# Attention with rotary embedding: rotated rows are transposed unstacked and spread by DMA, TensorE's steps are evened, GpSimd forms the cosine product from batch 1 on

## The chip, the cores and the metric

The kernel runs on one core of a Trainium2 chip. The metric is the device time of one execution in microseconds (us).

## What is computed

The program is a chain of two blocks, each an attention and a feed-forward part. The change lies in the first attention alone: four batches (B = 4) of 512 tokens (S = 512) with a width of 256, as 16 heads of 16 dimensions.

```
qkv = (x @ Wqkv + bqkv).reshape(b, s, 3, H, hd)
q, k, v = (qkv[:, :, 0], qkv[:, :, 1], qkv[:, :, 2])
...
def rot(t):
    t1, t2 = jnp.split(t.astype(jnp.float32), 2, axis=-1)
    return jnp.concatenate([t1 * c - t2 * si, t1 * si + t2 * c], axis=-1).astype(x.dtype)
q = rot(q)
k = rot(k)
scores = jnp.einsum('bthd,bshd->bhts', q, k * scale)
attn = jax.nn.softmax(scores + causal_mask, axis=-1)
ctx = jnp.einsum('bhts,bshd->bthd', attn, v).reshape(b, s, d)
return ctx @ Wout + bout
```

## The kernel before

Everything named here is in `attention_stage`. Each engine has a program of its own, written out by hand; semaphores tie them together. After a start-up for batch 0, all engines walk through one common numbering of steps `t`, 96 steps for the scores (`ALL`) and a few more for what trails. A pair of heads (a window `w`) takes three steps, a batch takes eight windows, so `WIDTH` = 24 steps; `u` is the step within the batch. In step `t`:

- TensorE multiplies one third of a window's scores (`scores`, into two PSUM banks, one for each head of the pair), VectorE adds the causal mask and takes the negative row maxima (`maxima`). `scores` of a head waits until the maxima of that head's previous step are taken.
- Seven steps later (`LAG`) TensorE multiplies the scores again, transposed, with the shift by the maximum as a 49th row of the contraction (`shifted`); ScalarE exponentiates them (`exponentials`), GpSimd zeroes what lies above the diagonal (`keep_causal`, one step later), and TensorE weighs the values (`weigh`, in two of every six steps).
- Beside it the next batch is prepared (`front`): transposing the normalised tokens (`turn_x`), `project_qk` and `project_v` (seven matmuls each), rotary embedding (`rope_a`, `swapped`, `rotate`). The batch before is finished (`tail`): `turn_sums`, `normalise_sums`, `turn_context`, `project_half`, `add`.

Products keep nearly fp32 precision by a split: a number is a high part (fp32r) and a low rest, and a head's contraction of 48 rows holds (high, low, high) of q against (high, high, low) of k. Before the change these 64-wide stacks are made ahead of the transposition: ScalarE writes the high parts (`high`), GpSimd the rests (`low`), into `q_stack` and `k_stack`; VectorE's maxima go into column 48 of `q_stack`. `turn_stack` then transposes four blocks of 128x128 for each of three things in a window: q without its shift (`turn_q1`), k (`turn_k`), and q again with its shift (`turn_q2`). ScalarE copies q out of PSUM twice (`out_q1`, `out_q2`), VectorE copies k (`out_k`).

The SP queue in this stage only loads rows at its start and stores `x` and the normalised rows.

## Time and profile before

| | us |
|---|---|
| median of 3 runs | 1167.31 (1165.92 to 1172.52) |
| profiled execution, its time | 1165.93 |
| its span, first to last instruction | 1164.0 |
| TensorE busy, whole span | 1052.2 |
| first scores of the attention loop issued at | 236.65 |

The span is what the rows below share as a time axis; the time of an execution is slightly longer than its span. "Busy" on TensorE includes the modelled tail of a matmul, in which the next one already streams, so the mean duration of a matmul is not its price: the price is the distance from one start to the next.

### The profile page before, as it was taken

What the parts mean: (1) busy time and instruction counts of PE and PEld (TensorE: products, weight loads), DVE (VectorE), ACT (ScalarE), POOL (GpSimd) and SP (SyncE); (2) the same over time, 40 slices, a digit from 0 to 9 for tenths busy, and PEclk for the clock granted to TensorE, in tenths of its full rate; (3) what the DMA queues carried; (4) which work ended last, traced back from release to release, by engine and by line L of the source; (5) the groups of instructions that cost most, each with busy time, mean ns of one, the idle gap of its engine ahead of it and who ended that gap; (6) DMA issues with size and microseconds to landing.
All of it is one profiled execution on the core that took longest, in us unless ns stands there. A gap on an engine that the chain in (4) does not pass through costs nothing. (4 is left out here: it accounts for less than half of the span.)

```text
span 1164.0 us, 18769 instructions
## 1 busy us (share of the span) xinstructions
PE 1052.2 (90%) x6537; PEld 870.1 (75%) x6537; DVE 731.1 (63%) x1754; ACT 463.2 (40%) x806; POOL 432.6 (37%) x474
## 2 busy tenths in 40 slices
PE   4899995779999999987999987999988998899997
PEld 3778884656566665666888886888878897788886
DVE  7934443787777778557454446765648878555653
ACT  4324331327666756625243322233334434223222
POOL 3056654326362723201576521000139788300000
PEclk8699998889989998887999998999997999999999
DMA  9034422300000000117472241000010030000000
GB/s 335 31 94 144 156 80 90 108 0 2 2 1 20 1 19 19 37 37 290 143 252 91 83 162 61 1 1 1 1 73 1 4 70 1 1 1 19 19 19 19
DMA packets 36881, 72.39 MB, mean 62 GB/s; under 512 B 8180, under 2 KB 25654, under 8 KB 36536
## 3 DMA queue, kind: packets, MB, share of 16 engines
q1 hardware_dynamic: 29112, 50.21, 12.8%
q0 software_dynamic: 7680, 20.98, 5.5%
q8 instruction: 57, 0.93, 0.3%
q14 instruction: 32, 0.26, 0.1%
HBM read 47.04 MB, written 24.13 MB: 61 GB/s over the span
## 5 line engine op out<-in xcount | busy, mean ns | idle before, releaser
L2041 PE MATMUL ps<-xt,w 128*128 128x512 f32 x768 | 192.5, 401 | 7.0 <-PEq L66 7.0
L2041 PEld LDWEIGHTS ps<-xt,w 128*128 128x128 f32 x768 | 143.3, 192 | 36.9 <-issue 5.5
L1740 DVE CUSTOM_DVE_ANT_0 ps<-ps,att_mask 128x128 f32<-128x128 f32 (+3 forms) x256 | 119.1, 516 | 40.6 <-PE ps L1343 40.3
L718 PE MATMUL ps<-moe_w,moe_narrow_xb 128*128 x480 | 125.0, 395 | 0.0
L122 POOL TENSOR_TENSOR var_eps<-bn,eps 128x4 f32<-128x4 f32 x24 | 6.6, 275 | 290.5 <-DVE bn L99 265.5
L2137 DVE TENSOR_TENSOR had_gated<-ps,had_sig 128x512 f32<-128x512 f32 x64 | 44.3, 691 | 110.8 <-ACT had_sig L2094 110.8
L2094 ACT ACTIVATE had_sig<-ps 128x512 f32<-128x512 f32 x64 | 38.3, 598 | 188.7 <-PE ps L2041 188.7
L616 POOL DMA_INDIRECT moe_xs<-xn_rows,moe_index x80 | 80.7, 1009 | 75.5 <-DVE moe_index L1017 44.1
L622 POOL DMA_INDIRECT made_rows<-moe_units_made,moe_index x80 | 79.6, 994 | 74.6 <-ACT moe_units_made L845 62.1
L718 PEld LDWEIGHTS ps<-moe_w,moe_narrow_xb 128*128 128x128 f32 x480 | 90.1, 188 | 19.6
L1606 ACT ACTIVATE att_early_probs<-ps 128x384 f32<-128x384 f32 (+1 forms) x192 | 90.7, 527 | 29.4 <-PE ps L1358 28.5
L1245 POOL TENSOR_SCALAR_AFFINE_SELECT att_early_probs<-att_early_probs 128x256 f32<-128x256 f32 x128 | 53.5, 431 | 118.1 <-ACT att_early_probs L1606 118.0
L1036 DVE TENSOR_TENSOR moe_narrow_xb<-ps,moe_narrow_xb 128x512 fp32r<-128x512 f32 x40 | 27.6, 691 | 110.2 <-ACT moe_narrow_xb L827 110.1
L2055 PE MATMUL ps<-w,had_yhi 128*128 128x256 f32 x512 | 94.4, 283 | 1.8 <-DVE had_ylo L2149 1.8
L2055 PEld LDWEIGHTS ps<-w,had_yhi 128*128 128x128 f32 x512 | 82.9, 189 | 7.8 <-DVE had_ylo L2149 2.6
L827 ACT ACTIVATE moe_narrow_xb<-ps 128x512 fp32r<-128x512 f32 x40 | 23.8, 598 | 135.0 <-PE ps L702 135.0
L1343 PE MATMUL ps<-att_kt,att_q 48*128 48x256 f32 (+3 forms) x256 | 66.4, 417 | 11.8 <-DVE att_q_stack L1740 9.1
L2055 PE MATMUL ps<-w,had_ylo 128*128 128x256 f32 x256 | 72.2, 282 | 0.0
L2277 POOL TENSOR_TENSOR fea_inv_norm<-fea_norm,neg_half 128x24 f32<-128x24 f32 x16 | 66.7, 4172 | 11.3 <-DVE fea_norm L2506 11.1
L337 PE MATMUL ps<-column,ident 128*128 128x128 f32 x356 | 53.5, 320 | 18.3 <-PEq L66 11.1
L744 PE MATMUL ps<-moe_w,moe_units_yb 128*128 x480 | 67.6, 280 | 0.0
L337 PEld LDWEIGHTS ps<-column,ident 128*128 128x128 f32 x356 | 51.7, 234 | 19.8 <-issue 11.2
(276 smaller groups left out, 2320.0 us busy)
## 6 DMA issues: line engine op xcount, KB each, us to landing
moe_w<-in_moe SPq DMA_DIRECT2D x16, 768.0 KB, 8.9
back<-made_rows SPq DMA_DIRECT2D x16, 512.0 KB, 5.7
x<-x_turned SPq DMA_DIRECT2D x8, 512.0 KB, 7.9
low_weights<-moe_w SPq DMA_DIRECT2D x4, 768.0 KB, 3.6
moe_w<-low_weights SPq DMA_DIRECT2D x4, 768.0 KB, 16.7
x<-in_x SPq DMA_DIRECT2D x4, 512.0 KB, 5.5
xn_rows<-moe_wide_xn SPq DMA_DIRECT2D x4, 512.0 KB, 10.7
x_turned<-x SPq DMA_DIRECT2D x4, 512.0 KB, 2.9
```

The source lines that it names most:

```text
L337: nc.tensor.matmul(g.ps[:, bank, 0:P], g.ident[:, :], g.column[:, :], start=True, stop=True)
L616: nc.gpsimd.indirect_dma_start(out=xs[:, j % AHEAD, i, :], out_offset=None, in_=g.xn_dram[:, :], in_offset=at(0, 2 * j + i)).then_inc(gath ...
L622: nc.gpsimd.indirect_dma_start(out=g.made_dram[:, :], out_offset=at(1, 2 * j + i), in_=made[:, j % 2, i, :], in_offset=None) \
L718: last = nc.tensor.matmul(h_bank(j, i), xb[a][:, j % 2, i, k, :], weight(c), start=False, stop=(k == KC - 1 and c == 1))
L744: last = nc.tensor.matmul(O_BANK[:, i * D:(i + 1) * D], yb[a][:, j % 2, i, c, :], weight(q), start=False, stop=(c == IC - 1 and q == 1), s ...
L1245: last = nc.gpsimd.affine_select(block, block, [[0, 2], [1, P]], ALU.is_ge, 0.0, base=0, channel_multiplier=-1)
L1343: last = nc.tensor.matmul(g.ps[:, a, col:col + n], q1[at, w % 2, i * P:n], kt[at, w % 4, 0:n], start=True, stop=True)
L1606: nc.scalar.activation(probs[:, w % 3, a, at:at + n], g.ps[:, 2 + a, 0:n], ACT.Exp, scale=HD ** -0.5).then_inc(exp_done, 1)
L1740: last = nc.vector.tensor_tensor_reduce(g.ps[:, a, col:col + n], g.ps[:, a, col:col + n], mask[:, SEQ - n:SEQ], -1.0, 3.0e38, ALU.add, ALU ...
L2041: last = nc.tensor.matmul(g.ps[:, bank(n, half), :], w[a][:, k, c * P:(c + 1) * P], xt[low][:, b % 2, k, :], start=(k == 0 and q == 0), st ...
L2055: last = nc.tensor.matmul(o, a[:, n % 4, at], g.w2[w][:, c, :], start=(c == 0 and q == 0 and i % 2 == 0), stop=(c == HC - 1 and q == 2), s ...
L2277: nc.gpsimd.tensor_tensor(inv_norm[:, t % 4, :], norm2[:, t % 4, :], g.neg_half[:, 0:QKH], ALU.pow) \
```

## The change

The rotated rows stay as they are (`rot`, 128 tokens x 512 columns for each of four token tiles). A chunk is 128 columns of them, that is eight heads of q or of k, so a batch has four chunks (q and k of heads 0 to 7, q and k of heads 8 to 15). `turn_chunk` transposes a chunk as it is (four blocks of 128x128), ScalarE takes the high part and VectorE the rest (`high_chunk`, `low_chunk`) into `stage`, SP stores both to DRAM (`store_chunk`, two DMAs) and loads them back spread over the 48 rows of the two heads of each pair (`load_chunk`, six DMAs), into `qt` and `kt`. The first pair's rows of batch 0 are placed from `stage` directly. The maxima go into a small tile `shift`; four matmuls with an identity turn them into two rows (`turn_shift`), ScalarE copies these out (`out_shift`), and SP places each into row 48 of `qt` (`place_shift`, two DMAs for a window). `shifted` waits for that landing. `WIDTH`, `LAG` and the products themselves stay.

Besides, projections are cut in pieces over several steps, `weigh` splits three blocks to one instead of two to two, `project_v` fills one PSUM bank with two tiles, and from batch 1 on GpSimd forms the product with the cosines, in place in `qk`, behind its two products with the sines. In batch 0 GpSimd takes the sine products, which VectorE took before, and VectorE keeps the cosine product. The ones in `kt` are set by two GpSimd memsets of 4096 columns (`set_ones`), the second behind the sine products of batch 0. Norm statistics of batch `b + 2` move from step 19 to step 5, their use from 22 to 7; `store_x` and `store_xn` of batches 0 and 1 move to fixed steps in SP's list.

```diff
-        rot = turns("rot", [P, 2, 2 * D])
...
-        part_b = sb("part_b", [P, 2, 2 * D])
+        rot = sb("rot", [P, BT, 2 * D])
+        stage = sb("stage", [P, 2, 2, SEQ], F32R)
+        shift = sb("shift", [P, 3, BT, 2], F32R)
+        shift_row = sb("shift_row", [P, SEQ], F32R)
+        ident_r = sb("ident_r", [P, P], F32R)
         v = sb("v", [P, 2, BT, H, HD + 1])
-        q_stack = sb("q_stack", [P, 2, BT, H, SK], F32R)
-        k_stack = sb("k_stack", [P, 2, BT, H, SK], F32R)
-        q1 = sb("q1", [P, 2, SEQ], F32R)
-        q2 = sb("q2", [P, 2, SEQ], F32R)
-        kt = sb("kt", [P, 4, SEQ], F32R)
+        qt = sb("qt", [P, 2, H // 2, SEQ], F32R)
+        kt = sb("kt", [P, 2, H // 2, SEQ], F32R)
         inv_sum = sb("inv_sum", [P, BT, H])
...
+        COPIES = ((0, 1, 0), (0, 0, 1))
+        CHUNK_BANK = 4
+        LEAD_CHUNKS = 2
+        stacked = (qt, kt)
+
+        CHUNK_TURNS = {2: 2, 5: 3}
+        for b in range(1, BATCH):
+            begin = WIDTH * (b - 1)
+            CHUNK_TURNS.update({begin + 17: 4 * b, begin + 18: 4 * b + 1, begin + 23: 4 * b + 2, begin + 26: 4 * b + 3})
+
...
+        def shift_turned_at(t):
+            return (t - 4) // STEPS if t >= 4 and (t - 4) % STEPS == 0 and (t - 4) // STEPS < BATCH * PAIR else None
...
+            def store_chunk(n):
+                b, c = n // 4, n % 4
+                sp.wait_ge(chunk_hi, n + 1)
+                sp.wait_ge(chunk_lo, n + 1)
+                if b:
+                    sp.wait_ge(rows_here[c], 96 * b)
+                for half in range(2):
+                    sp.dma_start(g.spread_dram[c, half], f32(stage[:, n % 2, half, :])).then_inc(stage_stored[n % 2], 16)
+
+            def load_chunk(n):
+                b, c = n // 4, n % 4
+                begin = 1 if n < LEAD_CHUNKS else 0
+                sp.wait_ge(stage_stored[n % 2], 32 * (n // 2 + 1))
+                sp.wait_ge(ones_set, min(b, 1) + 1)
+                if b >= 2:
+                    sp.wait_ge(st_ps, 2 * STEPS * PAIR * (b - 1))
+                for a, rows, half in copies(n):
+                    mine = g.spread_dram[c, half].rearrange("(m a d) n -> a d m n", a=2, d=HD)[a]
+                    sp.dma_start(f32(stacked[n % 2][rows, b % 2, 4 * (c // 2) + begin:4 * (c // 2) + 4, :]),
+                                 mine[:, begin:, :]).then_inc(rows_here[c], 16)
+
+            def place_shift(w):
+                b, hp = w // PAIR, w % PAIR
+                sp.wait_ge(shift_out, w + 1)
+                for a in range(2):
+                    at = 64 * a + 3 * HD
+                    sp.dma_start(f32(qt[at:at + 1, b % 2, hp, :]), f32(shift_row[a:a + 1, :])).then_inc(shift_here, 16)
...
+            for t in range(ALL + LAG):
+                if shift_turned_at(t - 1) is not None:
+                    place_shift(shift_turned_at(t - 1))
+                if t - 2 in CHUNK_TURNS:
+                    load_chunk(CHUNK_TURNS[t - 2])
+                if t - 1 in CHUNK_TURNS:
+                    store_chunk(CHUNK_TURNS[t - 1])
+                if t in BESIDE:
+                    store, b = BESIDE[t]
+                    store(b)
...
+                if n >= BT:
+                    pool.wait_ge(b_done, n + 1)
+                    heads = qk[:, n % 2, :].rearrange("p (h d) -> p h d", d=HD)
+                    nc.gpsimd.tensor_tensor(heads, heads, rope_c[:, n % BT, :].unsqueeze(1).to_broadcast([P, 2 * H, HD]),
+                                            ALU.mult).then_inc(a_done, 1)
...
-            def low(n):
-                pool.wait_ge(hi_done, n + 1)
-                b, i = n // BT, n % BT
-                halves = rot[:, n % 2, :].rearrange("p (s h d) -> p s h d", s=2, d=HD)
-                for s, (stack, hi, lo) in enumerate(((q_stack, 0, 1), (k_stack, 0, 2))):
-                    last = nc.gpsimd.tensor_tensor(stack[:, b % 2, i, :, lo * HD:(lo + 1) * HD], halves[:, s, :, :],
-                                                   f32(stack[:, b % 2, i, :, hi * HD:(hi + 1) * HD]), ALU.subtract)
-                last.then_inc(lo_done, 1)
...
+            def turn_rows(n, i):
+                kind, half = n % 2, n % 4 // 2
+                at = kind * D + half * P
+                return nc.tensor.transpose(g.ps[:, chunk_bank(n), i * P:(i + 1) * P], rot[:, i, at:at + P], g.ident[:, :])
+
...
+            def turn_shift(w, t):
+                pe.wait_ge(cleared, 2)
                 pe.wait_ge(max_done, 2 * STEPS * (w + 1))
+                pe.wait_ge(chunk_hi, chunks_turned(t))
+                pe.wait_ge(chunk_lo, chunks_turned(t))
+                if w:
+                    pe.wait_ge(shift_out, w)
+                for i in range(BT):
+                    last = nc.tensor.matmul(g.ps[0:2, CHUNK_BANK, i * P:(i + 1) * P], shift[:, w % 3, i, :],
+                                            ident_r[:, :], start=True, stop=True)
+                last.then_inc(shift_ps, 1)
...
-                    pe.wait_ge(q2_out, w + 1)
+                    pe.wait_ge(shift_here, 32 * (w + 1))
...
+            for i in range(BT):
+                project_v(0, i, 5 + i // 2)
+                pe.wait_ge(rot_done, i + 1)
+                for n in range(LEAD_CHUNKS):
+                    last = turn_rows(n, i)
+                    if i == BT - 1:
+                        last.then_inc(chunk_ps, 1)
+            spin(nc, g, 1, 13)
+            pe.wait_ge(chunk_lo, LEAD_CHUNKS)
...
+                        weigh((t - 14) // 6, 1)
                     elif (t - 14) % 6 == 1:
-                        weigh((t - 14) // 6, 1)
                         weigh((t - 14) // 6, 0)
-                if step == 0 and s + 1 < BATCH * PAIR:
-                    turn_q1(s + 1)
-                elif step == 1 and s + 1 < BATCH * PAIR:
-                    turn_k(s + 1)
-                elif step == 2 and 1 <= s <= BATCH * PAIR:
-                    turn_q2(s - 1)
...
-                        project_qk(front, 0, 6)
+                        project_qk(front, 0, 6, range(0, 1))
                     elif u == 4:
-                        project_qk(front, 1, 5)
+                        project_qk(front, 0, 6, range(1, 4))
+                    elif u == 5:
+                        project_qk(front, 0, 6, range(4, 7))
+                        project_qk(front, 1, 5, range(0, 3))
+                    elif u == 6:
...
+                if shift_turned_at(t) is not None:
+                    turn_shift(shift_turned_at(t), t)
+                if t in CHUNK_TURNS:
+                    turn_chunk(CHUNK_TURNS[t], t)
...
+            def high_chunk(n):
+                act.wait_ge(chunk_ps, n + 1)
+                if n >= 2:
+                    act.wait_ge(stage_stored[n % 2], 32 * (n // 2))
+                if LEAD_CHUNKS <= n < 2 * LEAD_CHUNKS:
+                    act.wait_ge(direct_here[n % 2], 96)
+                nc.scalar.activation(stage[:, n % 2, 0, :], g.ps[:, chunk_bank(n), :], ACT.Copy).then_inc(chunk_hi, 1)
+
+            def out_shift(w):
+                act.wait_ge(shift_ps, w + 1)
+                if w:
+                    act.wait_ge(shift_here, 32 * w)
+                nc.scalar.activation(shift_row[0:2, :], g.ps[0:2, CHUNK_BANK, :], ACT.Copy).then_inc(shift_out, 1)
...
-            def out_k(w):
-                dve.wait_ge(k_ps, w + 1)
-                if w >= 4:
-                    dve.wait_ge(st_ps, 2 * STEPS * (w - 3))
-                nc.vector.tensor_copy(kt[:, w % 4, :], g.ps[:, 4, :]).then_inc(k_out, 1)
+            def low_chunk(n):
+                dve.wait_ge(chunk_hi, n + 1)
+                nc.vector.tensor_tensor(stage[:, n % 2, 1, :], g.ps[:, chunk_bank(n), :], f32(stage[:, n % 2, 0, :]),
+                                        ALU.subtract).then_inc(chunk_lo, 1)
...
+                if t - 1 in CHUNK_TURNS:
+                    low_chunk(CHUNK_TURNS[t - 1])
```

TensorE in batch 2, from the last weighing of a group of heads in step `u` = 3 on (`L1373`/`L1454` weigh, `L1343`/`L1422` are scores, `L1358`/`L1439` shifted scores, `L1294`, `L1297`/`L1362`, `L1365` a projection). Before:

```order
L1373 MATMUL ps<-att_early_probs_4139,att_v 17x512 x4
L1313 MATMUL ps<-ident,att_q_stack 128x128 x4
L1294 MATMUL ps<-att_b_row,ones 128x512
L1297 MATMUL ps<-wqkv0,att_xt0 128x512
L1297 MATMUL ps<-wqkv1,att_xt0 128x512
L1297 MATMUL ps<-wqkv0,att_xt1 128x512
L1297 MATMUL ps<-wqkv0,att_xt0 128x512
L1297 MATMUL ps<-wqkv1,att_xt0 128x512
L1297 MATMUL ps<-wqkv0,att_xt1 128x512
L1343 MATMUL ps<-att_kt,att_q1 128x384 x2
L1358 MATMUL ps<-att_q2,att_kt 128x512 x2
L1313 MATMUL ps<-ident,att_k_stack 128x128 x4
```

After, from the same place (`L1401` is `turn_shift`):

```order
L1454 MATMUL ps<-att_early_probs_4139,att_v 17x512 x4
L1362 MATMUL ps<-att_b_row,ones 128x512
L1422 MATMUL ps<-att_kt,att_qt 128x384 x2
L1439 MATMUL ps<-att_qt,att_kt 128x512 x2
L1365 MATMUL ps<-wqkv0,att_xt0 128x512
L1365 MATMUL ps<-wqkv1,att_xt0 128x512
L1365 MATMUL ps<-wqkv0,att_xt1 128x512
L1401 MATMUL ps<-att_ident_r,att_shift 2x128 x4
L1422 MATMUL ps<-att_kt,att_qt 128x512 x2
L1439 MATMUL ps<-att_qt,att_kt 128x384 x2
L1365 MATMUL ps<-wqkv0,att_xt0 128x512
L1365 MATMUL ps<-wqkv1,att_xt0 128x512
```

The transposes of `q_stack` and `k_stack` are gone, a projection that stood whole in one step is spread over three, and four matmuls with two columns (`att_shift`) are new.

The SP queue between its loads and the end of the stage. Before:

```order
L330 DMA back_49<-made_rows 128x4x256 x6
L1182 DMA x_turned0<-x 128x4x256 x2
L1186 DMA xn_rows<-att_turns_after_xn_4143 128x4x256 x2
L1182 DMA x_turned0<-x 128x4x256
L1186 DMA xn_rows<-att_turns_after_xn_4143 128x4x256
```

After, from the rows of maxima in batch 0 that follow its own chunks to the first steps of batch 2 (`spread_rows` is the DRAM tensor, `att_shift_row` the row of maxima):

```order
L1235 DMA att_qt<-att_shift_row 1x16x32 x10
L1216 DMA spread_rows<-att_stage 128x512 x2
L1227 DMA att_qt<-spread_rows 16x4x512 x6
L1216 DMA spread_rows<-att_stage 128x512 x2
L1235 DMA att_qt<-att_shift_row 1x16x32 x2
L1227 DMA att_kt<-spread_rows 16x4x512 x6
L1235 DMA att_qt<-att_shift_row 1x16x32 x2
L1216 DMA spread_rows<-att_stage 128x512 x2
L1227 DMA att_qt<-spread_rows 16x4x512 x6
L1235 DMA att_qt<-att_shift_row 1x16x32 x2
L1239 DMA x_turned0<-x 128x4x256
L1216 DMA spread_rows<-att_stage 128x512 x2
```

Where SP had only stores that nothing in the loop waits for, it now issues in one list the chunks' stores and loads and the rows of maxima; a load waits for its store to land, and what stands behind it waits with it.

## Rows read from the trace of the kernel before

**Rows 1.** The page, part 1: busy time of each engine, whole span.
```profile
PE 1052.2 (90%) x6537; PEld 870.1 (75%) x6537; DVE 731.1 (63%) x1754; ACT 463.2 (40%) x806; POOL 432.6 (37%) x474
```

**Rows 2.** Windows: the fourth batch of the attention loop, and the loop whole.
```profile
core 0: us, PE busy (x) PEld busy (x) DVE busy (x) ACT busy (x) POOL busy (x), PEclk, DMA share, GB/s
...
420.00:480.00 60.00, 57.27 (x419) 35.19 (x411) 46.72 (x181) 34.85 (x71) 15.69 (x38) 0.89 0.08 28
237.00:481.70 244.70, 231.40 (x1627) 151.19 (x1626) 186.54 (x662) 152.50 (x312) 98.80 (x176) 0.92 0.03 10
```

**Rows 3.** Waits inside the loop, 237 to 481.7 us: waiter, awaited, us, times, longest.
```profile
DVE ps L1740 <- PE ps L1343: 40.3, 35, 3.5
...
PE ps L1343 <- DVE att_q_stack L1740: 9.1, 19, 3.1
```

**Rows 4.** Groups of instructions, 215 to 520 us.
```profile
L1313 PE MATMUL ps<-ident,att_q_stack 128*128 128x128 f32 x256 | 45.6, 305 | 1.8 <-DVE att_kt L1730 1.3
...
L1313 PE MATMUL ps<-ident,att_k_stack 128*128 128x128 f32 x128 | 22.4, 301 | 1.1 <-ACT att_q L1590 0.7
L1730 DVE CAST att_kt<-ps 128x512 fp32r<-128x512 f32 x32 | 21.9, 685 | 1.4 <-PE ps L1313 1.3
L1225 POOL TENSOR_TENSOR att_part_b<-att_qk,att_rope_s 128x256 f32<-128x256 f32 x24 | 20.5, 875 | 16.0 <-ACT att_qk L1566 16.0
...
L1590 ACT ACTIVATE att_q<-ps 128x512 fp32r<-128x512 f32 x32 | 19.2, 599 | 33.6 <-PE ps L1313 33.6
...
L1716 DVE TENSOR_TENSOR att_turns_rot<-att_qk,att_rope_c 128x512 f32<-128x512 f32 x16 | 12.2, 762 | 3.4 <-ACT att_qk L1566 3.4
...
L1708 DVE TENSOR_TENSOR att_xt<-ps,att_xt 128x512 fp32r<-128x512 f32 x6 | 4.1, 686 | 1.8 <-ACT att_xt L1558 1.8
```

**Rows 5.** Timeline of TensorE, four pieces in batch 1.
```profile
309.44 0.66 PE L1313 MATMUL ps<-ident,att_k_stack 128*128 128x128 f32 x4
309.85 0.48 PE L1294 MATMUL ps<-att_b_row,ones 128*128 128x512 f32 x1
310.17 1.56 PE L1297 MATMUL ps<-wqkv,att_xt 128*128 128x512 f32 x6
311.65 0.50 PE L1343 MATMUL ps<-att_kt,att_q 48*128 48x512 f32 x2
```

**Rows 6.** Windows: two neighbouring stretches of the loop, and one around rows 5.
```profile
268.00:271.40 3.40, 2.56 (x18) 1.83 (x16) 3.36 (x10) 1.91 (x5) 3.40 (x6) 0.94 0.00 0
271.40:274.80 3.40, 3.40 (x17) 2.68 (x16) 2.40 (x11) 2.19 (x6) 2.58 (x5) 0.56 0.00 0
308.80:312.20 3.40, 3.40 (x20) 2.23 (x19) 2.41 (x7) 2.12 (x4) 1.44 (x2) 1.00 0.00 0
```

**Rows 7.** Timeline at the start-up: VectorE, GpSimd and the first scores.
```profile
208.48 1.79 DVE L1804 SCALAR_TENSOR_TENSOR x<-back,route,x 128x256 f32<-128x256 f32 x4
...
230.95 4.31 DVE L1804 SCALAR_TENSOR_TENSOR x<-back,route,x 128x256 f32<-128x256 f32 x4
...
232.05 2.53 POOL L1215 TENSOR_TENSOR x<-x,att_bout 128x1024 f32<-128x1024 f32 x1
...
236.65 0.50 PE L1343 MATMUL ps<-att_kt,att_q 48*128 48x128 f32 x4 [0.88 <-DVE att_kt L1730]
```

**Rows 8.** DMA issues: KB each, us from issue to landing.
```profile
back<-made_rows SPq DMA_DIRECT2D x16, 512.0 KB, 5.7
...
low_weights<-moe_w SPq DMA_DIRECT2D x4, 768.0 KB, 3.6
...
x_turned<-x SPq DMA_DIRECT2D x4, 512.0 KB, 2.9
...
route<-route_rows SPq DMA_DIRECT2D x1, 16.0 KB, 1.9
```

**Rows 9.** Timeline of the SP queue: one DMA issued.
```profile
485.21 0.36 SPq L1182 DMA_DIRECT2D x_turned<-x  x1
```

376 lines of the change are left out of this document (167 added, 209 removed).

## Prediction

> **What bounds the kernel now.** I read the page's busy shares first: TensorE is busy for 1052.2 of 1164.0 us [rows 1]. That is an average over stages, and the change touches one, so the next view is the windows of that stage. The attention loop, from the first maxima to the last, takes 244.7 us for 96 steps, 2.55 us a step; in it TensorE is busy for 231.4 us, VectorE for 186.5, ScalarE for 152.5, GpSimd for 98.8 [rows 2]. The waits say who waits for whom: VectorE's maxima wait 40.3 us for scores, TensorE's scores wait only 9.1 us for maxima [rows 3]. So TensorE is what ends last in most steps, and VectorE, busy for 76% of the loop, is next. The granted clock averages 0.92 over the loop [rows 2], that is, a part of it runs at 1.2 instead of 2.4 GHz. A reader should see two things here: work taken from TensorE counts, and it counts only until VectorE, or a wait that is new, is last.
>
> **What TensorE loses.** 256 transposes of the q stack and 128 of the k stack go [rows 4]. Their mean of 0.3 us is not their price, since matmuls overlap: four transposes start at 309.44 and the next matmul at 309.85, so one costs 0.41 / 4 = 0.103 us [rows 5], at a granted clock of 1.00 [rows 6]. 384 x 0.103 = 39.4 us at full clock, 42.8 at the loop's 0.92.
>
> **What TensorE gains.** 64 transposes of chunks, 56 of them inside the loop: 56 x 0.103 = 5.8 us. 128 matmuls for the shift, 128 columns moving and 2 columns of weights, which the trace does not show. Above they are bounded by the transpose (0.103), below by the streaming of 128 columns: six matmuls of 512 columns take 311.65 - 310.17 = 1.48 us [rows 5], 0.247 each, a quarter of which is 0.062. I take 0.062, since the weights are short: 7.9 us (13.2 at most). Together 13.7 us, 14.9 at 0.92. Net: 42.8 - 14.9 = 27.9 us less (22 at least).
>
> **Does VectorE take over?** It loses 32 copies of k at 0.685 us, 21.9 us, and 12 cosine products at 0.762, 9.1 us, and gains 14 rests of a chunk in the loop, which I cost as the rests of x at 0.686, 9.6 us [rows 4]. That is 21.4 us less, 165.1 us of work. In a loop of 244.7 - 27.9 = 216.8 us its share is 76%, as before, so the full cut should show unless something new waits. ScalarE trades 64 copies of 0.6 us [rows 4] for 32 of the rows of maxima and 14 of chunks, and drops the writing of the stacks; it has room and I cost it at nothing. Its cover is that it sits idle for a third of the loop.
>
> **New wait one: chunks through PSUM.** A chunk is turned at the end of a step; ScalarE's copy takes 0.60 us, VectorE's rest 0.69 [rows 4], and in VectorE's list that rest stands ahead of the step's maxima, for which the next scores wait. So VectorE stands for 0.60 us and then works 0.69 us ahead of the maxima. A step will be about 216.8 / 96 = 2.26 us long and TensorE has its own work in it. Bounds: nothing, or all 1.29 us for 14 chunks, 18 us. I take 0.3 us each, 4 us, because one step of slack lies between scores and maxima.
>
> **New wait two: SP's list.** Nothing in the loop hung on SP before; now `shifted` waits for a row of maxima placed by DMA. Undisturbed, the row needs 0.60 for the copy, two issues at 0.36 each [rows 9] and 1.9 to land (a 16 KB transfer [rows 8]), 3.2 us from the end of the step that turned it. It is wanted two steps and the next scores later, after some 4.6 us. So it is hidden with 1.4 us to spare. A load of a chunk is six issues, 2.2 us, and it waits until the chunk's store (512 KB, 2.9 us [rows 8]) has landed, so some 5 us after the turn; the row of maxima then queues behind six issues and is 2.2 - 1.4 = 0.8 us late. By the order of SP's list this happens about three times in each of three batches: 7 us, of which I count 6. Below: nothing. Above: if a row landed only after 5.7 us as the loads of `back` do [rows 8], every window would be 2.4 us late, 77 us. I stay near the low end because 16 KB is the row nearest in size to 2 KB.
>
> The Trainium skill speaks against this placing. "DMA: Bandwidth & Descriptors", section "Queues, rings and completion order", says that one issuing engine's transfers lie in one ring for each DMA engine and are taken in ring order. No row of before has a small transfer behind a large one, so no run here shows it yet. By that rule the row would be held by the load's data too, and the sum would be the one of the rival "the loads hold the rows" below instead of mine.
>
> **New wait three: GpSimd's cosine product.** Sine products are two at 0.875 us [rows 4]. The cosine product of 512 columns is not in the trace: half of the bias addition over 1024 columns (2.53 us [rows 7]) is 1.27, two sine products are 1.75. I take 1.3, so 3.05 us a token tile. VectorE's `rotate` comes two steps after the start for the first two tiles (4.5 us, hidden) but one step (2.26 us) after it for the third, and waits about 0.8 us there with the maxima behind it; the fourth has two steps again but stands behind the third on GpSimd. Three batches x about 1 us: 3 us, between 0 and 9.
>
> **Start-up.** VectorE loses the sine products of batch 0, and the chain through high and low stacks goes. In its place come two copies, two rests, and direct placing by DMA (six issues and a landing, 2.2 + 1.9 = 4.1 us). That lies beside work which VectorE has anyway: statistics and the adding of batch 2's rows. This adding took 4.31 us beside GpSimd's bias addition, against 1.79 us for the same four instructions with GpSimd idle [rows 7]. The first scores came at 236.65 [rows 7]. I expect them 2 us earlier; bounds 5 us earlier, if the adding escapes GpSimd, and 4 later, if the memset of 4096 columns slows it again.
>
> **Evening and clock.** Evening can win back at most the 9.1 us that scores wait for maxima [rows 3]; I take 4. Against it stands the clock. After a stretch of 3.4 us in which TensorE was busy for 2.56, the next one shows 0.56 [rows 6], so 3.4 us of it at 1.2 GHz, a loss of about 1.7 us of full-clock work. A lighter TensorE will idle more often; two or three such stretches more cost 4 us. The two cancel.
>
> **The sum.** -27.9 + 4 + 6 + 3 - 2 = -16.9 us. The profiled execution took 1165.93 us, 1.4 below the median of 1167.31. So about 1149 against the former, 1150 against the median.
>
> **Rivals.**
> - The clock recovers (0.12). What is left is denser in real products, and in batch 3 of the loop, with no projections, the clock was 0.89 [rows 2], so there is room. At full clock the loop would be 0.08 x 217 = 17 us shorter: 1133. Against it: idling comes before the drops [rows 6], and there will be more. The Trainium skill, "TensorE: Matmul & The Clock Gate", section on transposes, says that transposes do not count as activity for the gate as other matmuls do; by that rule, which no row here isolates, this rival is what would happen.
> - The loads hold the rows (0.18). A row of maxima lands no sooner than the load ahead of it: 2.2 us of issue and 3.6 for 768 KB [rows 8] make 5.8 instead of 2.2 + 0.72 + 1.9 = 4.8, so 1 us more in nine places, 9 us; VectorE's in-order waits at the upper half of their bounds look alike. Time 1159.
> - Slower (0.12). The place is `shifted` at the first step of a window, waiting for its row. At a landing of 3.3 us or less it is hidden; at 4.4 us, between the 3.6 of a 768 KB transfer and 5.7 [rows 8], each of 32 windows is 1.1 us late, 35 us on 1150: 1185. The gain of 17 us is used up at a landing of 3.9 us in every window. Against it: the small transfer at 1.9 us.
> - What remains is my forecast (0.58).
>
> **Range and chances.** My own case spans 1140 to 1160. To hold 8 in 10, I reach down to the clock's 1133 and up past the held rows to 1163; the slower case and a tail below stay out. About 0.5% (1161.5 to 1173) is what a measurement of this kernel can tell from no change. Faster: 0.58 + 0.12 + 0.10 of the held rows = 0.80. Same: 0.08, the rest of these. Slower: 0.12.
>
> **What the profile after would show.** Transposes of stacks absent and TensorE's busy time about 25 us less in a loop of about 225 to 230 us. Shift matmuls starting 0.06 us apart if I am right, 0.10 if not. A wait of `shifted` for a DMA of `att_qt`, some nine times and about 1 us each; 32 times means the slower rival, never means that I overcounted. VectorE waiting for GpSimd at the third tile's `rotate`. Rests of chunks with an idle time of 0.6 us ahead of them. The granted clock between 0.88 and 0.93; above 0.97 the first rival. Wrong would make it above all a landing of small rows that is far from 1.9 us, or a start-up in which the direct placing, not VectorE, is last.

## The result and the profile after

The changed kernel took 1197.88 us (median; 1196.26 to 1199.83), the kernel before 1169.91 us beside it (1165.92 to 1175.57). The ratio is 1.0236, 95% interval 1.0185 to 1.0287: slower by 28 us, where I had predicted 1150. The profiled execution took 1198.74 us.

The page of the changed kernel, part 1, answers to [rows 1]:

```profile
PE 1051.4 (88%) x6347; PEld 854.0 (71%) x6347; DVE 713.0 (60%) x1719; ACT 435.0 (36%) x750; POOL 430.1 (36%) x460
```

TensorE has 190 matmuls fewer and is as busy as before. The windows say why. First the four batches of the attention loop in the kernel before, each from its first maxima to those of the next, the last to the end of its last maxima (a batch has 64 of them), and then the loop whole (columns as in [rows 2]: length, busy time of PE, PEld, DVE, ACT and POOL, granted clock, DMA share, GB/s):

```profile
237.70:297.63 59.93, 53.67 (x323) 35.12 (x322) 47.81 (x167) 34.90 (x70) 25.00 (x41) 0.89 0.00 1
297.63:363.19 65.56, 63.23 (x471) 42.93 (x472) 49.33 (x171) 42.65 (x90) 30.22 (x52) 0.95 0.01 1
363.19:427.98 64.79, 62.82 (x466) 42.38 (x466) 46.40 (x159) 42.55 (x89) 28.89 (x49) 0.95 0.03 9
427.98:483.82 55.84, 53.10 (x381) 32.15 (x381) 44.24 (x171) 33.78 (x69) 15.10 (x36) 0.88 0.09 30
237.70:483.82 246.12, 232.82 (x1638) 152.58 (x1638) 187.79 (x665) 153.88 (x315) 99.21 (x177) 0.92 0.03 10
```

The cuts of [rows 2], 420 to 480 us for the fourth batch and 237 to 481.7 for the loop, lie some us before these; busy shares agree within 0.01 in the loop, and the clock there is the same 0.92. The same stretches in the changed kernel:

```profile
236.76:305.96 69.20, 54.95 (x287) 32.42 (x288) 44.99 (x160) 29.02 (x57) 24.72 (x37) 0.70 0.52 101
305.96:374.46 68.50, 60.48 (x425) 36.39 (x422) 46.51 (x163) 36.68 (x76) 28.48 (x47) 0.88 0.38 71
374.46:445.87 71.41, 59.57 (x412) 35.71 (x412) 42.35 (x152) 35.76 (x75) 27.42 (x46) 0.88 0.41 82
445.87:507.85 61.98, 52.09 (x330) 28.10 (x331) 41.12 (x165) 28.76 (x61) 14.26 (x35) 0.72 0.28 69
236.76:507.85 271.09, 227.10 (x1450) 132.62 (x1451) 174.97 (x636) 130.21 (x268) 94.88 (x164) 0.80 0.40 81
```

The loop went from 246.1 to 271.1 us. Every batch took longer, with less work on VectorE and ScalarE, at a lower clock. The last two columns are new too: the DMA engines are busy for two fifths of the loop, against 0.03 in [rows 2].

The two profiled spans differ by 33.0 us, and the loop holds 25.0 of them. Another 9.0 lie behind the loop (680.2 against 689.2 us), in stages that the change doesn't touch; the last section returns to them.

The waits of the changed kernel in its loop, 234 to 506 us (waiter, awaited, us, times, longest), answer to [rows 3]:

```profile
ACT att_early_probs L1683 <- PE ps L1439: 92.4, 47, 6.6
DVE ps L1808 <- PE ps L1422: 48.4, 32, 6.1
...
PE ps L1439 <- DMA att_qt<-att_shift_row: 24.1, 7, 5.1
...
DVE att_stage L1798 <- ACT att_stage L1667: 16.4, 13, 3.3
...
PE ps L1422 <- DVE att_shift L1808: 12.0, 25, 2.0
...
DVE att_rot L1793 <- POOL att_qk L1308: 3.1, 2, 1.5
```

The third shown is new: `shifted` (L1439) stood for a row of maxima seven times, 3.4 us each. I had expected nine times and 1 us. What hangs on TensorE stood with it: ScalarE's exponentials waited 92.4 us.

One of the seven stalls. The SP queue's timeline of the changed kernel (start, us, engine, line, operation):

```profile
425.90 2.67 SPq L1227 DMA_DIRECT2D att_qt<-spread_rows  x6
428.68 0.83 SPq L1216 DMA_DIRECT2D spread_rows<-att_stage  x2
429.56 1.13 SPq L1235 DMA_DIRECT2D att_qt<-att_shift_row  x2
```

TensorE's timeline of the same place (in brackets, the idle time ahead of the row and what ended it):

```profile
425.50 0.44 PE L1401 MATMUL ps<-att_ident_r,att_shift 128*2 128x128 f32 x4
425.87 0.97 PE L1422 MATMUL ps<-att_kt,att_qt 48*128 48x512 f32 x2
...
431.71 0.44 PE L1422 MATMUL ps<-att_kt,att_qt 48*128 48x384 f32 x1 [0.19 <-DVE att_shift L1808]
436.31 0.80 PE L1439 MATMUL ps<-att_qt,att_kt 49*128 49x512 f32 x2 [4.16 <-DMA att_qt<-att_shift_row]
```

The shift was turned at 425.50. SP's list stood at a load of a chunk (six issues) and a store (two), so the two issues of the row began at 429.56 and not near 426.5. Then `shifted` began at 436.3, 6.7 us after the row's first issue, for 2 KB a DMA. The last of the row's two DMAs landed 6.2 us after its issue; with nothing ahead of it such a DMA lands after 1.6 to 1.7 us.

The seven stalls are alike. From the end of ScalarE's copy to the first issue a row stood 1.7 to 4.4 us in SP's list, 2.6 on average; from its second issue to its landing it took 4.1 to 6.2 us, 5.0 on average. The windows of the stall at 436.31 and of another, which ends at 265.52:

```profile
429.00:436.00 7.00, 2.76 (x19) 1.24 (x18) 3.29 (x15) 1.47 (x3) 0.76 (x2) 0.98 0.75 134
259.80:265.50 5.70, 3.58 (x13) 2.21 (x12) 4.45 (x18) 1.64 (x4) 3.06 (x4) 0.50 0.67 79
```

In the first the DMA engines were busy for 75% of the time, at 134 GB/s. The source view of the place gives the row's issues (ns min/median/max) and their landing:

```profile
L1235 SPq DMA_DIRECT2D att_qt<-att_shift_row x64: 497/564/1135, 250.3 to 513.5; - x64
...
DMA to landing us min/median/max: 1.6/2.3/6.2
```

Groups of the changed kernel, 215 to 545 us, for the operations that I had to bound:

```profile
L1300 POOL TENSOR_TENSOR att_rot<-att_qk,att_rope_s 128x256 f32<-128x256 f32 x32 | 24.4, 783 | 11.5 <-ACT att_qk L1651 11.5
...
L1401 PE MATMUL ps<-att_ident_r,att_shift 128*2 128x128 f32 x128 | 16.3, 259 | 0.4 <-DVE att_stage L1798 0.4
L1308 POOL TENSOR_TENSOR att_qk<-att_qk,att_rope_c 128x512 f32<-128x512 f32 x12 | 15.4, 1282 | 0.9
...
L1798 DVE TENSOR_TENSOR att_stage<-ps,att_stage 128x512 fp32r<-128x512 f32 x16 | 11.0, 690 | 17.5 <-ACT att_stage L1667 17.5
```

### The profile page after: what moved, and what is told of

The parts are those of the page before. It is cut to its first block and busy times, and to the rows that moved or that the text cites. A ratio compares the mean times of both kernels' runs of the same rounds, so it can differ in the third digit from the quotient of the medians.

```text
span 1197.0 us, 18461 instructions
## 1 busy us (share of the span) xinstructions
PE 1051.4 (88%) x6347; PEld 854.0 (71%) x6347; DVE 713.0 (60%) x1719; ACT 435.0 (36%) x750; POOL 430.1 (36%) x460
## 5 line engine op out<-in xcount | busy, mean ns | idle before, releaser
L719 PE MATMUL ps<-moe_w,moe_narrow_xb 128*128 x480 | 127.7, 402 | 0.0
L1316 POOL TENSOR_SCALAR_AFFINE_SELECT att_early_probs<-att_early_probs 128x256 f32<-128x256 f32 x128 | 55.9, 450 | 164.3 <-ACT att_early_probs L1683 164.3
L1422 PE MATMUL ps<-att_kt,att_qt 48*128 48x256 f32 (+3 forms) x256 | 73.4, 463 | 22.1 <-DVE att_shift L1808 12.0
L1422 PEld LDWEIGHTS ps<-att_kt,att_qt 48*128 48x128 f32 x256 | 35.2, 217 | 62.7 <-DVE att_shift L1808 32.4
L1439 PE MATMUL ps<-att_qt,att_kt 49*128 49x128 f32 (+3 forms) x256 | 55.1, 380 | 25.4 <-DMA att_qt<-att_shift_row 24.1
## 6 DMA issues: line engine op xcount, KB each, us to landing
moe_w<-low_weights SPq DMA_DIRECT2D x4, 768.0 KB, 16.4
```

The costliest lines, as they stand in the source:

```text
L719: last = nc.tensor.matmul(h_bank(j, i), xb[a][:, j % 2, i, k, :], weight(c), start=False, stop=(k == KC - 1 and c == 1))
L1316: last = nc.gpsimd.affine_select(block, block, [[0, 2], [1, P]], ALU.is_ge, 0.0, base=0, channel_multiplier=-1)
L1422: last = nc.tensor.matmul(g.ps[:, a, col:col + n], qt[at, b % 2, hp, i * P:n], kt[at, b % 2, hp, 0:n], start=True, stop=True)
L1439: last = nc.tensor.matmul(g.ps[:, 2 + a, col:col + n], kt[at, b % 2, hp, j * P:(j + 1) * P], qt[at, b % 2, hp, j * P:SEQ], start=True, sto ...
```

## The experiments

Theory A: a row stands behind a chunk's transfers, and that costs the stall and the lower clock behind it. Rivals: the issue list alone; the cosine product or the evening; the clock by itself. E1, E2, E3, E4 are edits of the changed kernel; E5 to E8 followed from them, E9 to E15 from those. Each comparison was beside the kernel before, which lay between 1167.7 and 1170.4 us (medians).

For the main ones, the median time beside two stretches of the profiled execution: the loop, from the start of the first maxima to the end of the last, and what lies behind it.

| | median, us | loop, us | behind the loop, us |
|---|---|---|---|
| before | 1169.91 | 246.1 | 680.2 |
| changed | 1197.88 | 271.1 | 689.2 |
| E8 (one execution) | 1187.83 | 268.7 | 681.8 |
| E2 | 1166.18 | 245.8 | 688.6 |
| E5 | 1171.10 | 253.5 | 689.1 |
| E7 | 1159.22 | 236.4 | 685.1 |
| E12 | 1170.01 | 247.4 | 681.1 |

The last column moves by 9 us with the same code in it, so the loops are the better comparison between two traces, the medians between two kernels.

**E1 and E8, the rows on ScalarE's queue.** `place_shift` goes from SP's list to ScalarE, right behind the copy of the row:

```diff
-                if shift_turned_at(t - 1) is not None:
-                    place_shift(shift_turned_at(t - 1))
...
+                act.wait_ge(shift_out, w + 1)
...
+                for a in range(2):
+                    at = 64 * a + 3 * HD
+                    nc.scalar.dma_start(f32(qt[at:at + 1, b % 2, hp, :]), f32(shift_row[a:a + 1, :])) \
+                        .then_inc(shift_here, 16)
```

> The changed kernel, but ScalarE itself issues the two DMAs of a row of maxima, right behind its copy, so they no longer stand behind a chunk's load in SP's queue. Everything else stays. Theory A (the rows land late because they share SP's queue with the loads; each lateness idles TensorE and costs clock behind it): the seven waits of shifted scores for the row, 24 us, shrink to under 5 us, the loop's granted clock rises from 0.79 to about 0.88, and the time falls from 1198 to 1155-1168 us. Theory B (a thinner TensorE is throttled whatever the rows do): the waits shrink alike, but the clock stays at 0.80-0.82 and the time ends at 1172-1178. Theory C (the DMA engines themselves are full of the load's packets, so another queue does not help): waits stay above 15 us and the time above 1190. ScalarE pays some 1.2 us a window for issuing; it has room.

Measured: 1195.86 us, ratio 1.0227 (1.0194 to 1.0260). The rows below are from E8, one more execution of the same kernel:

> The kernel of the ScalarE queue once more, for a trace at the usual clock. It took 1196, as the changed kernel did. If the other queue does not help because the DMA engines are full of the load, rows land 5 to 6 us after their issue from ScalarE too, and shifted scores wait some 24 us for them. If rows land in under 3 us, something else must have taken the gain: ScalarE's issuing, 2 x 0.6 us a window ahead of its exponentials.

It took 1187.83 us. Waits of E8, 234 to 500 us:

```profile
PE ps L1413 <- issue: 15.7, 3, 8.4
...
PE ps L1430 <- DMA att_qt<-att_shift_row: 2.9, 4, 1.2
```

And from the view of the row's tile, its issues, who waited for them and the landing:

```profile
L1669 ACTq DMA_DIRECT2D att_qt<-att_shift_row x64: 504/570/1151, 250.9 to 511.3; - x64
...
  ACT att_early_summed L1687: 15.5, 12
...
DMA to landing us min/median/max: 1.6/2.0/5.5
```

The waits for late rows are nearly gone (24.1 to 2.9 us), and the loss is not. What went is the stand in SP's list: every row is now issued 0.03 us after its copy. The slow landing stayed. In the seven windows that had stalled, the row took 4.1 to 5.1 us from its second issue, against 4.1 to 6.2 on SP's queue, and over the whole stage 24 of 64 DMAs took more than 3.5 us in either kernel. In 14 windows of each, loads or stores from SP's queue were in flight when the row was issued, and the row landed behind all of them, also when it came from ScalarE's queue. So another queue doesn't carry a row past the bulk, and none of the three theories above held as a whole.

Two new costs took the place of the old one. ScalarE spends 0.57 us on each issue, and its own next work stood behind them, 15.5 us in the group shown. And the scores that open a batch stood 8.39, 4.04 and 3.31 us (at 305.9, 372.1 and 443.2 us) at their wait for the batch's first chunks; the last load of these landed 0.1 us before each. The opening waits alone don't explain it, since E5 below has 15.2 us of them in a loop that is 15 us shorter. ScalarE's issues are what is left, and no run tests them by themselves.

**E2, the turned step earlier.** The rows of maxima are turned one step sooner (at t = 3, 6, ... in place of 4, 7, ...), and so are the first two chunks of a batch:

```diff
-            CHUNK_TURNS.update({begin + 17: 4 * b, begin + 18: 4 * b + 1, begin + 23: 4 * b + 2, begin + 26: 4 * b + 3})
+            CHUNK_TURNS.update({begin + 16: 4 * b, begin + 17: 4 * b + 1, begin + 23: 4 * b + 2, begin + 26: 4 * b + 3})
-            return (t - 4) // STEPS if t >= 4 and (t - 4) % STEPS == 0 and (t - 4) // STEPS < BATCH * PAIR else None
+            return (t - 3) // STEPS if t >= 3 and t % STEPS == 0 and (t - 3) // STEPS < BATCH * PAIR else None
```

> The changed kernel, but a window's maxima are turned one step earlier (three steps after its first instead of four), which gives each row one more step, about 2.5 us, before it is wanted; the first two chunks of a batch are turned at steps 16 and 17 instead of 17 and 18, so that the shared PSUM bank is free. Rows still stand behind the loads in SP's queue. Theory A: waits of 2 to 5 us each lose about 2.5 us each, so from 24 to 6-10 us, and the time falls to 1165-1180. Theory B: waits fall alike, the clock stays near 0.80, and the time is 1180-1185. Theory C: as A, since more slack helps whatever holds the row.

Measured: 1166.18 us, ratio 0.9987 (0.9958 to 1.0016), 31.7 us under the changed kernel by the medians. Waits of E2 in its loop:

```profile
DVE ps L1808 <- PE ps L1422: 30.1, 28, 3.6
...
PE ps L1439 <- DMA att_qt<-att_shift_row: 1.3, 1, 1.3
```

One step of slack takes away the wait for rows and with it all of the loss; its loop is 25.3 us shorter than that of the changed kernel, 22.8 of which are this wait.

**E3, the cosine product back on VectorE.** `rope_a` stands in VectorE's list again, ahead of each `rotate`.

> The changed kernel with one part undone: from batch 1 on the product with the cosines is VectorE's again, directly ahead of its sum, instead of GpSimd's. If GpSimd's product costs what I predicted (3 us of waits) and VectorE's takes 0.76 us x 12 = 9 us of an engine that is not last, the time moves by less than 4 us either way (1194-1202). A theory in which GpSimd's product is the main loss would give under 1190.

1195.35 us, ratio 1.0210 (1.0148 to 1.0272): the same as the changed kernel. Its `shifted` waited 23.4 us for rows, 9 times. GpSimd's product was not the cause.

**E4, the projections whole again** (the evening undone): `project_qk(front, 0, 6)` at u = 3 in place of pieces at 3, 4 and 5, and so on.

> The changed kernel with the evening undone: projections of q and k whole in steps 3, 4, 7 and 8 and the weighing two blocks to two, as before the change. I predicted 4 us for the evening, so 1198 + 4 = 1202 if that holds. If evening is worth nothing: within 2 us of 1198. If the pieces cost the clock (TensorE thin in each step instead of full in some): below 1194 and a higher granted clock in the loop.

1194.13 us, ratio 1.0204 (1.0165 to 1.0242): the same again, with 23.0 us of waits for rows. Neither was the evening the cause of the loss. (The profiled execution took 1203.87 us, 10 above the median, so its loop of 276.5 us says little about the evening.)

**E5, the loads in pieces.** A chunk's six loads are issued two by two on three steps, and the row of a step stands between them:

```diff
-                if t - 2 in CHUNK_TURNS:
-                    load_chunk(CHUNK_TURNS[t - 2])
+                for piece in range(2, -1, -1):
+                    if t - 2 - piece in CHUNK_TURNS:
+                        load_chunk(CHUNK_TURNS[t - 2 - piece], piece)
```

> The changed kernel, but a chunk's load is issued in three pieces of two DMAs, one piece a step, each behind the row of maxima of that step in SP's list. A row then has at most 256 KB of load just ahead of it instead of 768 KB. Rows are still turned at the same step. If a row is late because of the load ahead of it (queue or DMA engines), its landing falls from about 6 us to about 3, the waits of shifted scores from 24 us to under 6, and the time from 1197 to 1165-1172, as with the earlier turning. If something else holds the rows, it stays above 1185.

1171.10 us, ratio 1.0020 (0.9990 to 1.0051), 26.8 us under the changed kernel, with the same DMAs, bytes and arithmetic. Waits of E5, 234 to 490 us:

```profile
PE ps L1424 <- issue: 15.2, 3, 7.5
...
PE ps L1441 <- DMA att_qt<-att_shift_row: 2.4, 3, 1.4
```

In the seven windows that had stalled, the row now stood 0.15 to 3.0 us in the list and landed 1.8 to 3.3 us after its second issue, as was expected. (Elsewhere in this loop six DMAs of rows still took more than 3.5 us, the slowest 6.8, in windows where nothing waited for them. The profiled execution took 1180.92 us, 10 above the median.) E2 gives the row time, E5 takes the loads out of its way; both recover nearly all. That the rows stood behind the chunks' transfers, and that this made the loss, is shown from two sides. That the stalls also lowered the clock is hardly: it is 0.83 and 0.81 in the loops of E2 and E5, against 0.80. The first row is the price that E5 pays: the scores that open a batch wait 15.2 us for its chunks, where the changed kernel waited 3.9.

**E6, dummy work for the clock.** E2 with four products on constants (`spin(nc, g, CHUNK_BANK, 4)`, eight matmuls in the trace, 0.81 us from their start to the next at full clock) ahead of each window's shift matmuls.

> The kernel with the maxima turned one step earlier, with 4 idle products (fp32, 128x128x128, eight matmuls, about 0.5 to 0.9 us at full clock) added on TensorE ahead of each turning of the maxima: 32 x 0.5 to 0.9 = 15 to 29 us of useless work. Theory B (TensorE's clock fell from 0.92 to 0.83 in this loop because it has less to do between waits, and that eats what the removed transposes gave): the clock rises to 0.88 or more and the time stays within 5 us of 1166 or falls. Rival (the clock is no cause, TensorE's work and waits decide): the time rises by 12 us or more, to 1178 or above.

1179.04 us, ratio 1.0093 (1.0056 to 1.0130). The clock of the four batches went from 0.73, 0.91, 0.92 and 0.76 in E2 to 0.81, 0.96, 0.97 and 0.91, and the time rose by 13 us. The added work is 32 x 0.81 = 26 us at full clock, so about half of it was paid for by the better clock or lay in waits, and the rest was a loss. E2 itself had won back the loss at a clock of 0.83 in its loop, so the loss hung on the rows and not on the clock; what a higher clock without added work would bring, no run shows.

**E7, both: E2 and E5.**

> Both: maxima turned one step earlier and loads in pieces. If after the earlier turning rows still cost something (1 to 5 us of waits are left in its trace), this gives 1160-1164; if nothing of the rows is left, the same 1166 as the earlier turning alone.

1159.22 us, ratio 0.9887 (0.9853 to 0.9921): 10.6 us faster than the kernel before. No `shifted` waited for a row. The batches of E7:

```profile
236.00:300.66 64.66, 51.96 (x287) 31.61 (x288) 44.92 (x161) 29.15 (x57) 24.53 (x37) 0.74 0.56 109
300.66:361.26 60.60, 57.76 (x425) 35.32 (x424) 45.99 (x163) 36.47 (x76) 28.42 (x47) 0.92 0.41 80
361.26:417.26 56.00, 53.13 (x417) 32.23 (x415) 42.46 (x152) 35.87 (x75) 27.07 (x45) 1.00 0.50 105
417.26:472.42 55.16, 50.53 (x331) 26.07 (x328) 40.78 (x165) 30.21 (x63) 15.08 (x36) 0.78 0.32 78
```

The third batch, at a clock of 1.00, is 8.8 us shorter than before, the second, at 0.92, 5.0. The fourth, at 0.78, is only 0.7 shorter, and the first, at 0.74, is 4.7 longer. At the end of the first lies one long wait, 6.06 us of TensorE until 299.86, for the first chunks of the next batch; the last load of these landed at 299.76.

**E9, the list or the bytes?** From the third batch on each load brings a quarter of its bytes, with as many issues (those batches are computed partly from an older batch's rows):

```diff
+                    end = 4 if b < 2 else 1
-                                 mine[:, begin:, :]).then_inc(rows_here[c], 16)
+                                 mine[:, begin:end, :]).then_inc(rows_here[c], 16)
```

> From the third batch on (chunks 8 to 15) each load of a chunk brings one pair's rows in place of four: the same six issues on SP's list, at the same places, with a quarter of the bytes (32 in place of 128 KB each). The stores, the first two batches' loads and all arithmetic stay; the third and fourth batches are computed partly from rows of an older batch. If what holds the rows of maxima is the transfer ahead of them (theory A), the stalls of the maxima-row waits after about 340 us (three or four of the seven, 3 to 5 us each, and the lower clock behind them) go, those before it stay: 1180 to 1185. If it is the list itself (issues of 0.45 us, six at a time, 2.7 us: theory B), all seven stay, a little shorter: 1193 to 1198.

1179.34 us, ratio 1.0088 (1.0051 to 1.0126), just under the range of A. But both theories hold a share. The stalls of the changed kernel after 340 us, from TensorE's timeline:

```profile
366.11 0.50 PE L1439 MATMUL ps<-att_qt,att_kt 49*128 49x512 f32 x2 [2.11 <-DMA att_qt<-att_shift_row]
394.68 0.78 PE L1439 MATMUL ps<-att_qt,att_kt 49*128 49x512 f32 x2 [3.56 <-DMA att_qt<-att_shift_row]
...
465.97 0.79 PE L1439 MATMUL ps<-att_qt,att_kt 49*128 49x512 f32 x2 [5.07 <-DMA att_qt<-att_shift_row]
```

With the one shown above these are 14.9 us. Those of E9:

```profile
388.62 0.50 PE L1440 MATMUL ps<-att_qt,att_kt 49*128 49x512 f32 x2 [1.49 <-DMA att_qt<-att_shift_row]
426.31 0.80 PE L1440 MATMUL ps<-att_qt,att_kt 49*128 49x512 f32 x2 [1.61 <-DMA att_qt<-att_shift_row]
452.18 0.79 PE L1440 MATMUL ps<-att_qt,att_kt 49*128 49x512 f32 x2 [1.66 <-DMA att_qt<-att_shift_row]
```

4.8 us in three. In these three the row landed 1.7 to 2.0 us after its second issue, about as fast as one with nothing ahead of it, but it had stood 2.3 to 3.1 us in the list. So some 10 of 14.9 us are the data ahead of the row, and 1.6 us a stall are the list of issues, which the bytes do not touch.

**E10, E11 and E12, around E7.** E10 issues a chunk's loads three by three on two steps. E11 is E7 with the cosine product on VectorE, E12 is E7 with whole projections.

> The turned step one step earlier and a chunk's six loads in two groups of three, on two steps (the kernel of this pair measured before has three groups of two, on three steps, at 1159.2). The scores that open the second batch waited 6.06 us there (290 to 300 us: 16 DMA engines busy throughout, loads of 128 KB). If that wait ends with the last load's issue, one step earlier takes about 2 us off it: 1157. If it ends with the transfers, which take the same time in any order, the wait stays, and a row behind three loads comes up to 0.6 us later: 1159 to 1163.

> The version at 1159.2 (one step earlier, loads in pieces) with the cosine product back on VectorE. In the changed kernel, whose TensorE stood for the rows of maxima, moving it back took 2 us off. With the rows on time VectorE's path is nearer: 12 products of 0.65 us more on VectorE, against 12 of 1.28 us on GpSimd ahead of the rotation. If GpSimd is what keeps the rotated rows late (scores of the second batch wait 6.06 us for their chunk) the time falls by 1 to 4 us, to 1155 to 1158; if VectorE sets the maxima it rises by 2 to 6 us, to 1161 to 1165.

> The version at 1159.2 with the projections whole again, as in the kernel before (four steps of 2.9 us of projection, no pieces). My prediction gave the evening 4 us; in the changed kernel undoing it cost nothing (1194 beside 1198), where the late rows covered it. If evening is worth its 4 us once the rows are on time: 1163. If it is worth nothing: 1159, within 2.

E10: 1159.57 us, ratio 0.9900 (0.9866 to 0.9935); the opening wait of the second batch was 4.62 us in place of 6.06, but it ended no earlier (300.41 against 299.86), and the total stayed. E11: 1160.81, 0.9935 (0.9901 to 0.9970): no effect that its interval can tell from E7. E12: 1170.01, 1.0010 (0.9973 to 1.0047): the evening is worth 10.8 us by the medians (14 by the ratios, 11.0 in the loops) once the rows are on time, where in E4 the medians showed nothing of it. The wait that it shortens, VectorE for scores in E12's loop, 234 to 474 us, against 24.9 us in E7's:

```profile
DVE ps L1800 <- PE ps L1424: 40.9, 31, 4.8
```

**E13 and E14, dummy work only where the clock was low.** E7 with four, or two, products on constants a window (eight or four matmuls) in the first and fourth batch. (The lengths of batches in the first expectation come from cuts some us too early; by the maxima E6 against E2 is 2.4 and 0.2 us shorter in the first and fourth batch and 3.2 and 3.5 longer in the others.)

> The version at 1159.2 (turned step one step earlier, loads in pieces) with four matmuls on constants ahead of each window's shift matmuls, in the first and the fourth batch only, where its granted clock was 0.76 and 0.79; 0.92 us of work a window, 14.7 us in all. With them in every window of the one-step-earlier kernel the clock of these two batches had risen from 0.73 to 0.83 and from 0.77 to 0.91, and the batches took 3.5 and 0.3 us less, while the second and third took 5.2 and 3.8 us more. If the lower clock is where the rest of the computed gain went and can be had back, the two batches take 3 to 5 us less together: 1154 to 1156. If the work only costs what the clock returns: 1158 to 1161. If it costs more than that: over 1162.

> As the run beside it, with two such matmuls a window in place of four (7.4 us of work in all, in the first and fourth batch). If the clock answers to a little work as to much: 1153 to 1156. If the effects cancel: 1158 to 1161.

1167.25 us (0.9991, 0.9962 to 1.0021) and 1161.42 us (0.9930, 0.9905 to 0.9955). The two batches in E13:

```profile
238.89:303.14 64.25, 52.99 (x343) 34.92 (x344) 44.97 (x160) 29.17 (x57) 24.49 (x37) 0.87 0.57 113
424.58:484.40 59.82, 55.54 (x387) 34.26 (x384) 40.61 (x165) 29.90 (x61) 14.85 (x36) 0.80 0.30 72
```

The first ran at 0.87 in place of 0.74 and took 64.25 us in place of 64.66, with 56 matmuls more; the fourth ran at 0.80 in place of 0.78 and took 4.7 us longer. The clock can be had, but here the work that bought it cost as much as it gave, or more.

**E15, the rest of a chunk behind the maxima.** E7 with `low_chunk` after `maxima(t)` in VectorE's list:

> The version at 1159.2 with the rest of a chunk behind the step's maxima in VectorE's list, in place of ahead of them. There VectorE stood 15.4 us in all for ScalarE's copy of the chunk, in 10 of 14 steps, with the maxima behind it; my prediction gave this 4 us. If that wait lies on the path, the time falls by 4 to 12 us: 1147 to 1155. If another wait comes up in its place (the chunk's bank, its store and its loads all come up to 1.5 us later, and the scores that open the second batch already wait 6.06 us for theirs): 1157 to 1162.

1167.47 us, ratio 0.9982 (0.9952 to 1.0012): 8 us worse than E7, neither of the two times expected. Waits of E15, 234 to 480 us:

```profile
DVE ps L1810 <- PE ps L1424: 50.3, 40, 3.9
...
PE ps L1403 <- DVE att_stage L1800: 11.7, 11, 2.0
```

The second is the reason. Chunk and shift share PSUM bank 4, and `turn_shift` waits for `chunk_lo` before it may write there; the wait moved from VectorE, where it hid beside TensorE's work, onto TensorE itself.

## Why the prediction was wrong, point by point

**The step that failed** is "New wait two: SP's list", which gave 0.8 us of lateness in nine places, 6 us. The stand in the list came out near its estimate: 2.6 us on average in the seven stalls, against the 2.2 of six issues. An issue of such a row takes 0.56 us and not 0.36. The term that failed is the landing. It was costed at 1.9 us, as if the row were alone, and took 5.0 on average in the stalls, up to 6.2. Seven stalls made 24.1 us, 3.4 each in place of 0.8. I had written down the rival "the loads hold the rows" and priced it at 1 us a place: the row did land behind the load's data, and the size was a third of what was measured. My slower rival asked for a late landing in all 32 windows. Seven of them with 3.4 us each were enough. That the late rows made the loss is shown by E2 (31.7 us back) and E5 (26.8); E9 splits them into list and data.

In a sum: the time was 47.5 us above the forecast against the median, 1150.4. E7 gets back 38.7 us where 6 were costed for late rows, which is 32.7. E7 itself is 12.3 us short of the gain that my sum has without them, which stays open in the main (below). And the kernel before was 2.6 us slower beside the result than in the median I started from.

The Trainium skill's rule that I had cited against the placing, in "DMA: Bandwidth & Descriptors", section "Queues, rings and completion order" (SP's transfers lie in one ring for each DMA engine, ScalarE's in another), led to the right conclusion: on SP's queue every row landed behind the loads ahead of it. But these traces don't show that it is the shared ring that held it, since rows from ScalarE's queue landed behind SP's loads as well, after 4.1 to 5.1 us where the changed kernel had stalled. I weighed the rule with "a 16 KB row is the nearest in size". Size was the wrong likeness; what was in flight ahead of the row was the right one.

**The clock** was said to cost 4 us. It fell from 0.92 to 0.80 over the loop, and stood at 0.50, the lower of its two levels (1.2 GHz), from 259.8 to 265.5 us, around one stall. The first rival, that denser work would bring full clock, did not come about. It leaned on the Trainium skill's "TensorE: Matmul & The Clock Gate", Part 4 (PE-mode transpose), by which transposes are not activity for the gate as other matmuls are: with 384 transposes of the stacks gone the clock was lower, in the changed kernel (0.80) and in E7 (0.86 over its loop; 0.74, 0.92, 1.00 and 0.78 by batch) against 0.92. That doesn't refute the rule, because TensorE also idled more (23.0 us in E7's loop and 44.5 in the changed kernel's, against 10.5), and no run isolates the transposes.

**TensorE's net gain.** Shift matmuls start (425.87 - 425.50) / 4 = 0.093 us apart, not 0.062: 11.8 us for 128 and not 7.9. The term was 4 us too good. In E7's third batch the gain was 8.8 us, against a batch's share of 27.9 / 4 = 7.0; but the same batch took 64.07 us in E12, without the evening, at a clock of 0.87. So the 8.8 us are not the transposes' alone, and the net term is not measured by itself.

**Evening.** 4 us were costed; 10.8 by E12.

**Chunk rests.** 4 us were costed, at 0.3 us a place. VectorE stood 16.4 us in 13 places in the changed kernel, 15.4 in 10 in E7. How much of that lies on the path isn't shown, since E15 made another wait of it.

**GpSimd's cosine product** took 1.28 us (1.3 predicted), and `rotate` waited 3.1 us for it (3 predicted); E3 and E11 show no cost in the total.

**Start-up.** Scores began at 234.25 against 236.65 [rows 7], the 2 us predicted, after a wait of 2.92 us for `att_kt<-att_stage`: the direct placing was last, which I had named as a sign of being wrong. The first maxima came 0.9 us earlier, and the scores at 244.70 stood 2.32 us for `spread_rows`. Over E2, E7, E13 and E14, whose start-up is the same code, the first maxima lie between 236.0 and 239.2, so one profile doesn't resolve this term.

**What is left open.** With rows on time the change brings 10.6 us, where my sum without the late rows had 22.9 (16.9 + 6). Shift matmuls explain 4. E12 shows how much is missing: with rows on time and the projections whole, the kernel without 384 transposes took 1170.01 us beside 1168.28, and its loop 247.4 against 246.1. Of the 27.9 us that TensorE was to save nothing shows there; TensorE idled 26.9 us in that loop against 10.5, at a clock of 0.82 against 0.92. The gain came only together with the evening. By the batches of E7 the gain is missing in the first, which is 4.7 us longer than before, and in the fourth, which is 0.7 shorter. The first holds 3.36 us of waiting for batch 0's own spread rows (until 244.97) and the 6.06 us for those of the next batch, and its clock is 0.74; the clock of the fourth is 0.78. Dummy work for the clock (E6, E13, E14) or moving one wait (E10, E15) gave nothing back. How much is the clock and how much the chunks' loads is not settled.

## What to carry to other kernels

A small transfer on which an engine waits should be costed by what is ahead of it at that moment, first the issues in its list and then the bytes in flight, never by the landing of a transfer of its size elsewhere. Another queue took away the first part here and not the second, and charged the issues to an engine with work of its own. Giving the transfer a step of slack and cutting the bulk into pieces around it turned +2.4% into -1.1% with the same work. And undo the parts of a change again once its main fault is mended: the evening looked worthless beside the stalls and was worth 11 us without them.

## What the runs showed of the hardware that I had not expected

- A later stage that the change doesn't touch took different times at different clocks. With 424 matmuls in both, the windows of it in the kernel before and in the changed one are:

```profile
853.20:929.70 76.50, 70.64 (x424) 64.75 (x424) 56.92 (x109) 34.21 (x50) 59.98 (x23) 0.89 0.07 28
```

```profile
880.60:964.20 83.60, 77.37 (x424) 71.00 (x424) 55.68 (x108) 33.99 (x50) 59.74 (x23) 0.82 0.06 26
```

  E2 took 83.6 us there too, E3 78.5 and E8 77.8. So 7 us between two profiles can lie in a stage that the change doesn't touch, and a loop should be compared by its own marks. Whether this goes with the kernel or with the execution isn't shown, with one profile of each.
- A small DMA on the other queue did not overtake the bulk: in E8 a row of 2 KB issued by ScalarE landed behind every load and store that SP had in flight, in 14 windows of 14, after up to 5.5 us against 1.6 to 1.7 with nothing ahead of it.
- A chunk's loads and the store behind them kept the DMA engines 75% busy at 134 GB/s in the window shown, in rows of 2 KB; a load of 128 KB, issued in a group of six, landed after 4.1 us in the median (340 to 500 us).
- A DMA issue costs its engine 0.56 us on SP and 0.57 on ScalarE for this row of 2 KB, against 0.36 in [rows 9].
- GpSimd's sine product took 0.78 us, against 0.875 in [rows 4], with the same operands and another destination.
